# Score banks in a rotation of three, maxima by half in three single banks, values and side stages at exchanged steps

## Chip, cores and metric

One core of a Trainium2 chip runs the whole kernel. The metric is the device time of one execution in microseconds, over several runs; lower is better.

## What is computed

The input is 16 images of 128 channels by 32 x 32 pixels, fp32. Three blocks follow each other, each added to its input: a frequency-gated channel scaling, an attention over the 1024 pixels of an image (8 heads of 16, every token to every token, plus a fixed decaying mix over positions), and a mixture of 8 experts of which each token takes two. The change lies in the attention, which in the reference is:

```
qkvt = x @ W_qkv
q, k, v, t = map(to_heads, jnp.split(qkvt, 4, axis=-1))
dots = jnp.einsum('bhid,bhjd->bhij', q, k) * scale
attn1 = jax.nn.softmax(dots, axis=-1)
out1 = jnp.einsum('bhij,bhjd->bhid', attn1, v)
...
out2 = jnp.einsum('ij,bhjd->bhid', attn2, t)
return concatenated(out1, out2) @ W_out + b_out
```

The softmax subtracts each row's maximum before the exponential, so each row of 1024 dots is needed twice: once for its maximum, once for its exponentials.

## The kernel before

The program is written out by hand for five engines, each with its own instruction stream and semaphores between them. After a setup it runs one iteration `it` for each image, from -1 to 16, and each iteration has 64 **steps** `s`. The loop over steps stands once for each engine (L956 for TensorE, L1191 for ScalarE, L1552 for VectorE), and constants at L77 to L112 say at which step a stage is done. After that come 71 blocks of the expert stage and a closing sum, which the change leaves alone.

**Scores and exponentials.** Step `s` of image `it` has two score matmuls (`scores`, L867, matmul at L876), each of 128 keys by 512 queries of one head, with the negative maximum of the query as two more rows of the stationary and moving operand. They are written to two PSUM banks, `E_BANK + i` for i = 0, 1. ScalarE takes the exponential of each into `probs` in SBUF (`weights`, L1161, activation at L1167). TensorE issues the scores of step s + 1 within step s, and score i of a step waits until the exponential i of the step before is done (L875).

**Values.** Two steps make a **unit** of four heads. `values` (L880, matmuls at L890) multiplies the unit's four blocks of `probs` by the values of these heads, four matmuls on separate 32-column groups, and accumulates in bank 6 over eight units; ScalarE then copies the bank (`copy_o`, L1170). Values run at odd steps, behind the scores of the next step. At the seven steps of `AT_VALUES` they are split into two halves of 256 columns, one in the odd step and one in the even step after it.

**Maxima.** Forty steps ahead (`LEAD`), the scores are computed a first time with queries and keys exchanged (`full_scores`, L848, matmul at L855), 128 queries by 1024 keys in two halves of one bank each. Four banks hold two such units, `M_BANK + 2 * (n % 2) + c`. VectorE reduces the 1024 columns with one instruction (`maximum`, L1411, at L1417) into a column of `row_max`, and TensorE waits for the maximum two units back before it refills the banks (L854). A score and a half of the full scores lie in different row halves of the array, are issued one behind the other and run side by side; I call the two a **pair**. A step has two pairs.

When 32 units are done, `turn_maxima` (L861) transposes `row_max` on TensorE, VectorE negates and splits it (`shift`, L1420), and SyncE moves it with four DMAs into the row of the stacked queries (`load_shift`, L521). The scores of the group wait for that (L873): steps 0 and 32 of an image. `AT_MAX1` is the step at which the second group is turned, `AT_MAX0` that of the next image's first.

**Side stages.** One PSUM bank (`SIDE_BANK`, 7) serves all the other work of an image one after the other, in the order that `side_order` (L126) makes from the constants: transposes of x, the normalised x back, projections to q, k, v and z for the image after next or the next, transposes of the attention output, its projection, transposes for the second norm, gate logits, dispatch counts. TensorE does a stage at its step; ScalarE copies it out `LAG` = 2 steps later (one stage a step earlier), or VectorE reads it. VectorE also does scans for the position mix (`fade_forward`, `fade_backward`), moments, the choice of experts (`choose`, steps `AT_PICK`) and, on TensorE's logits, `logits_out` at `AT_LOGITS`. GpSimd normalises, splits q and k, and sends the tokens out by indirect DMA.

Each engine works strictly in the order of its stream, so a step's stage stands behind that step's pairs on TensorE, behind its exponentials on ScalarE and behind its maximum on VectorE.

## Time and profile before

| | us |
|---|---|
| median of 3 runs | 2412.41 |
| lowest, highest | 2411.95, 2437.68 |
| span of the profiled execution | 2663.0 |
| TensorE busy in it | 2213.5 |
| VectorE busy | 1836.0 |
| ScalarE busy | 1494.7 |
| GpSimd busy | 1021.2 |

Of the profiled execution no other time than its span is listed. The span goes from the first to the last instruction; what lies around it is not shown. It is 251 us longer than the median of the runs. Busy times are unions of what the profiler recorded; a matmul's end is modelled, and matmuls overlap, so TensorE's work is better read from the distance of successive starts. Images start about 117 us apart in it; the expert stage and the closing sum take the last 620 us.

### The profile page before, as it was taken

The page shows a single profiled execution, that of the slowest core. Times are in us where ns is not written, and L with a number is a line of the kernel's source. Part 1 is how long each engine was busy: PE and PEld are TensorE (multiplying, and loading weights), DVE is VectorE, ACT ScalarE, POOL GpSimd, SP SyncE. Part 2 cuts the span into 40 slices and gives each one's busy share as a digit, 9 for nine tenths or more (in the row PEclk, how much of TensorE's full clock was granted, in tenths as well). Part 3 has the DMA queues.
Part 4 walks back from the last instruction along what each step waited for, and adds up shares of the span by engine and source line. Part 5 has one row for each costly group of instructions (what it writes and reads, how often), then busy time and mean ns, then how long its engine had stood idle before and what let it go on. Part 6 is the DMA issues. An engine that isn't in the chain of part 4 may idle for free.

```text
span 2663.0 us, 35930 instructions
## 1 busy us (share of the span) xinstructions
PE 2213.5 (83%) x12448; PEld 985.6 (37%) x12448; DVE 1836.0 (69%) x2613; ACT 1494.7 (56%) x2897; POOL 1021.2 (38%) x1479
## 2 busy tenths in 40 slices
PE   2789998999989999998989999998897277676744
PEld 1333333333324333333434333333332255555633
DVE  5767887877878787888878778787731455555532
ACT  1147877767667676767767676766653033333320
POOL 2202224434241433424143432431404465655564
PEclk9969999989989898999999888898965588878765
DMA  5311223121222212122221212220102366555549
GB/s 167 55 25 25 36 55 89 34 49 40 45 51 51 58 29 54 36 47 48 56 59 29 53 36 47 43 55 26 49 1 93 121 231 191 168 161 168 167 139 345
DMA packets 100989, 215.11 MB, mean 81 GB/s; under 512 B 30224, under 2 KB 50392, under 8 KB 100376
## 3 DMA queue, kind: packets, MB, share of 16 engines
q1 hardware_dynamic: 78000, 166.96, 25.2%
q0 software_dynamic: 17280, 35.95, 3.9%
q10 hardware_dynamic: 5528, 9.91, 1.1%
q8 instruction: 99, 1.62, 0.3%
q14 instruction: 82, 0.67, 0.1%
HBM read 104.30 MB, written 61.23 MB: 62 GB/s over the span
## 4 chain that ended last, share of the span: by engine, by line
PE 63%; ACT 11%; another core or an unknown queue 7%; issue 7%; DMA 4%; POOL 4%; DVE 2%; SPq 1%; ACTq 1%; POOLq 0%; DVEq 0%
PE ps L876 27%; PE ps L890 19%; ACT region L1167 6%; PE ps L833 3%; DMA region<-y_dram 2%; PE ps L841 1%; PE ps L855 1%; PE ps L845 1%; PE ps L910 1%; PE ps L1019 1%; PE ps L1021 1%; POOL y_dram L763 1%; PE ps L923 1%; PE ps L899 1%
## 5 line engine op out<-in xcount | busy, mean ns | idle before, releaser
L1417 DVE TENSOR_REDUCE row_max<-ps 128x1 f32<-128x1024 f32 x1024 | 1235.4, 1216 | 347.2 <-PE ps L855 224.1
L1167 ACT ACTIVATE region<-ps 128x512 f32<-128x512 f32 x2048 | 1116.8, 596 | 566.1 <-PE ps L876 491.1
L876 PE MATMUL ps<-big 50*128 50x512 f32 x2048 | 889.8, 503 | 105.7 <-ACT region L1167 74.6
L855 PE MATMUL ps<-big 48*128 48x512 f32 x2048 | 887.7, 502 | 20.4 <-DMA big<-k_parts 14.8
L876 PEld LDWEIGHTS ps<-big 50*128 50x128 f32 x2048 | 361.2, 200 | 826.4 <-ACT region L1167 650.2
L890 PE MATMUL ps<-region 128*32 128x512 f32 (+1 forms) x4992 | 637.3, 586 | 0.7 <-ACT region L1167 0.7
L855 PEld LDWEIGHTS ps<-big 48*128 48x128 f32 x2048 | 362.7, 202 | 44.5 <-DVE row_max L1417 25.6
L763 POOL DMA_INDIRECT y_dram<-region x284 | 272.6, 960 | 201.5 <-ACT region L1251 123.0
L708 POOL DMA_INDIRECT xs_dram<-region,slot x256 | 249.7, 975 | 80.8 <-issue 71.7
L1019 PE MATMUL ps<-big 128*128 128x512 f32 x284 | 139.4, 491 | 110.9 <-DMA big<-w_dram 39.4
L693 POOL TENSOR_TENSOR region<-region 128x256 f32<-128x256 f32 x64 | 44.8, 732 | 446.1 <-DVE region L1463 446.1
L890 PEld LDWEIGHTS ps<-region 128*32 128x32 f32 x4992 | 102.4, 113 | 201.8 <-issue 200.4
L1243 ACT ACTIVATE region<-ps,big 128x512 f32<-128x512 f32 x71 | 49.0, 690 | 213.7 <-remote 132.1
L644 POOL TENSOR_TENSOR norm_v<-norm 128x8 f32<-128x8 f32 x32 | 6.8, 212 | 406.1 <-DVE norm L1407 406.1
L658 POOL TENSOR_TENSOR region<-region,norm_v 128x256 f32<-128x256 f32 x256 | 155.3, 638 | 6.6 <-POOL norm_v L652 2.9
L1634 DVE TENSOR_TENSOR big<-ps,big 128x512 fp32r<-128x512 f32 x71 | 48.9, 689 | 146.5 <-ACT big L1237 78.3
L1644 DVE TENSOR_SCALAR big<-ps,big 128x512 fp32r<-128x512 f32 x142 | 105.6, 744 | 62.8 <-remote 28.6
L1021 PE MATMUL ps<-big 128*128 128x512 f32 x284 | 127.9, 450 | 0.0
L1020 PE MATMUL ps<-big 128*128 128x512 f32 x284 | 127.8, 450 | 0.0
L1019 PEld LDWEIGHTS ps<-big 128*128 128x128 f32 x284 | 61.4, 216 | 148.4 <-ACT region L1243 60.5
L1647 DVE SCALAR_TENSOR_TENSOR big<-ps,big 128x512 fp32r<-128x512 f32 x142 | 106.6, 751 | 5.0
L1251 ACT ACTIVATE region<-ps,region 128x128 f32<-128x128 f32 x284 | 81.1, 374 | 27.5 <-remote 22.5
(182 smaller groups left out, 2019.2 us busy)
## 6 DMA issues: line engine op xcount, KB each, us to landing
big<-w_dram SPq DMA_DIRECT2D x71, 514.0 KB
big<-q_parts SPq DMA_DIRECT2D x384, 64.0 KB, 2.4
big<-k_parts SPq DMA_DIRECT2D x372, 64.0 KB, 2.4
region<-xs_dram SPq DMA_DIRECT2D x71, 264.0 KB
region<-y_dram SPq DMA_DIRECT2D x16, 1024.0 KB, 9.9
region<-in_x SPq DMA_DIRECT2D x28, 512.0 KB, 5.3
t_dram<-region SPq DMA_DIRECT2D x16, 512.0 KB, 3.4
out<-region ACTq DMA_DIRECT2D x16, 512.0 KB, 5.9
```

Of the source, the lines that this page charges most:

```text
L658: last = pool.tensor_tensor(some, some, v[:, row, t:t + 2].unsqueeze(2).broadcast_to([P, 2, P]), op)
L708: pool.indirect_dma_start(xs_dram[:, :], bass.IndirectOffsetOnAxis(ap=slot[:, n * TILES + t:n * TILES + t + 1], axis=0), n2_row[:, t, :], ...
L763: pool.indirect_dma_start(y_dram[:, :], bass.IndirectOffsetOnAxis(ap=xs[b % XS_BUFS][:, j, INDEX_COL:INDEX_COL + 1].bitcast(I32), axis=0), ...
L855: mm = pe.matmul(ps[:, M_BANK + 2 * (n % 2) + c, :], lane_rows(q_stack[k % 2], h, SHIFT_ROW)[:, t * P:(t + 1) * P], lane_rows(k_stack[k % ...
L876: pe.matmul(ps[:, E_BANK + i, :], lane_rows(k_stack[k % 2], h, STACK)[:, t * P:(t + 1) * P], lane_rows(q_stack[k % 2], h, STACK)[:, c * BA ...
L890: mm = pe.matmul(ps[32 * r:32 * r + 32, O_BANK, cols], v_aug[k % 2][:, t, g * GROUP + r, :], probs[:, u % 2, r, cols], start=(t == 0), sto ...
L1019: pe.matmul(dst, w[:, high_at:high_at + P], high, start=start, stop=False)
L1020: pe.matmul(dst, w[:, high_at:high_at + P], low, start=False, stop=False)
L1021: return pe.matmul(dst, w[:, low_at:low_at + P], high, start=False, stop=stop)
L1167: act.activation(probs[:, u % 2, step_head(k, s, i), :], ps[:, E_BANK + i, :], ACT.Exp, scale=DH ** -0.5).then_inc(exp_done, 1)
L1417: dve.tensor_reduce(row_max[:, h * TILES + t:h * TILES + t + 1], ps[:, at:at + 2, :], AX.XY, ALU.max).then_inc(max_done, 1)
L1647: dve.scalar_tensor_tensor(h_low[b % 2][f], src, w[:, NEG_B1 + f:NEG_B1 + f + 1], h_high[b % 2][f].bitcast(F32), ALU.max, ALU.subtract).th ...
```

## The change

The scores rotate through three banks (0 to 2), counted over all scores, and a score waits for the exponential three before it. The full scores rotate through three single banks (3 to 5), counted by half, and each half waits for the maximum three halves before it. VectorE reduces each half by itself into one of two columns, and joins the two columns with one `tensor_tensor` for each 32 units; `turn_maxima` waits for the join. Values run at even steps, whole, for the unit that ended with the step before, with a wait for its exponentials; the last unit of an image runs in step 0 of the next. Side stages move to odd steps, mostly one step later, some elsewhere; `LAG` is 1, and VectorE's moments keep their distance of 3 steps. The output copies move to the odd steps 17, 33, 49 and 1.

```diff
-AT_MAX1, AT_MAX1_FIRST = 26, 23
-AT_TURN_O3 = 4
-AT_BACK_O = (6, 8)
-AT_PREP = ((0, 2), (14, 16), (18, 20), (22, 24))
-AT_PREP_LATE = ((24, 26), (36, 38), (40, 42), (44, 46))
+AT_MAX1, AT_MAX1_FIRST = 27, 23
+AT_TURN_O3 = 5
+AT_BACK_O = (7, 9)
+AT_PREP = ((1, 3), (15, 17), (19, 21), (23, 25))
+AT_PREP_LATE = ((25, 27), (37, 39), (41, 43), (51, 55))
...
-AT_OUT = (32, 36)
+AT_OUT = (33, 37)
...
-AT_TURN_T2 = (42, 44)
-AT_LOGITS = 53
-AT_TURN_O = (48, 50, 52)
-AT_VZ = (54, 56, 58, 60)
-AT_VZ_FIRST = (24, 26, 28, 30)
-AT_DISPATCH = 62
-AT_VALUES = (10, 12, 28, 30, 38, 40, 46)
-LAG = 2
+AT_TURN_T2 = (41, 43)
+AT_LOGITS = 51
+AT_TURN_O = (31, 47, 53)
+AT_VZ = (45, 49, 59, 61)
+AT_VZ_FIRST = (27, 28, 29, 30)
+AT_DISPATCH = 63
+AT_COPY_O = (17, 33, 49)
+AT_COPY_O3 = 1
+LAG, MOMENT_LAG = 1, 3
...
-AT_GAP = 62
-AT_PICK = (54, 55, 56, 57, 58, 59, 60)
-AT_GATES = 63
-AT_AFFINE = 49
+AT_GAP = 60
+AT_PICK = (52, 53, 54, 55, 56, 57, 58)
+AT_GATES = 62
+AT_AFFINE = 48
...
-        row_max = sb("row_max", [P, STEPS])
+        row_max = sb("row_max", [P, HALVES, STEPS])
...
-        E_BANK, M_BANK, O_BANK, SIDE_BANK = 0, 2, 6, 7
+        E_BANK, M_BANK, O_BANK, SIDE_BANK = 0, 3, 6, 7
+        E_BANKS, M_BANKS = 3, 3
...
-                if unit >= 2:
-                    pe.wait_ge(max_done, unit - 1)
-                mm = pe.matmul(ps[:, M_BANK + 2 * (n % 2) + c, :],
+                half = HALVES * unit + c
+                if half >= M_BANKS:
+                    pe.wait_ge(max_done, half - M_BANKS + 1)
+                pe.matmul(ps[:, M_BANK + half % M_BANKS, :],
...
-                if c == HALVES - 1:
-                    mm.then_inc(full_ready, 1)
...
-                pe.wait_ge(max_done, k * STEPS + (g + 1) * GROUP_ROWS)
+                pe.wait_ge(max_joined, GROUPS * k + g + 1)
...
-                if k * STEPS + s:
-                    pe.wait_ge(exp_done, 2 * (k * STEPS + s) - 1 + i)
-                pe.matmul(ps[:, E_BANK + i, :], lane_rows(k_stack[k % 2], h, STACK)[:, t * P:(t + 1) * P],
+                score = 2 * (k * STEPS + s) + i
+                if score >= E_BANKS:
+                    pe.wait_ge(exp_done, score - E_BANKS + 1)
+                pe.matmul(ps[:, E_BANK + score % E_BANKS, :], lane_rows(k_stack[k % 2], h, STACK)[:, t * P:(t + 1) * P],
...
+                pe.wait_ge(exp_done, 2 * (k * STEPS + 2 * (u + 1)))
...
-                    if here and s % 2:
-                        values(it, s // 2, 0 if s + 1 in AT_VALUES else None)
-                    if here and s in AT_VALUES:
-                        values(it, s // 2 - 1, 1)
+                    if here and s and s % 2 == 0:
+                        values(it, s // 2 - 1)
+                    if post and s == 0:
+                        values(it - 1, UNITS - 1)
...
-                    act.activation(probs[:, u % 2, step_head(k, s, i), :], ps[:, E_BANK + i, :], ACT.Exp,
+                    score = 2 * (k * STEPS + s) + i
+                    act.activation(probs[:, u % 2, step_head(k, s, i), :], ps[:, E_BANK + score % E_BANKS, :], ACT.Exp,
...
-                    if s == 0 and post:
+                    if s == AT_COPY_O3 and post:
                         copy_o(it - 1, 3)
-                    if here and s in (16, 32, 48):
-                        copy_o(it, s // 16 - 1)
+                    if here and s in AT_COPY_O:
+                        copy_o(it, AT_COPY_O.index(s))
...
-                    for c, late in enumerate((LAG, LAG - 1)):
-                        if prep and s == at_k[c] + late:
-                            projected("k", it + 2, c, k_f, k_parts)
+                    if prep and s - LAG in at_k:
+                        projected("k", it + 2, at_k.index(s - LAG), k_f, k_parts)
...
-                dve.wait_ge(full_ready, k * STEPS + n + 1)
-                at = M_BANK + 2 * (n % 2)
                 h, t = max_unit(n)
-                dve.tensor_reduce(row_max[:, h * TILES + t:h * TILES + t + 1], ps[:, at:at + 2, :], AX.XY,
-                                  ALU.max).then_inc(max_done, 1)
+                for c in range(HALVES):
+                    half = HALVES * (k * STEPS + n) + c
+                    dve.wait_ge(full_ready, half + 1)
+                    dve.tensor_reduce(row_max[:, c, h * TILES + t:h * TILES + t + 1], ps[:, M_BANK + half % M_BANKS, :],
+                                      AX.X, ALU.max).then_inc(max_done, 1)
+                if (n + 1) % GROUP_ROWS == 0:
+                    rows = slice(n + 1 - GROUP_ROWS, n + 1)
+                    dve.wait_ge(max_done, HALVES * (k * STEPS + n + 1))
+                    dve.tensor_tensor(row_max[:, 0, rows], row_max[:, 0, rows], row_max[:, 1, rows],
+                                      ALU.max).then_inc(max_joined, 1)
```

## Rows read from the trace of the kernel before

**Rows 1.** Page, part 1: busy time, share of the span, instructions.
```profile
PE 2213.5 (83%) x12448; PEld 985.6 (37%) x12448; DVE 1836.0 (69%) x2613; ACT 1494.7 (56%) x2897; POOL 1021.2 (38%) x1479
```

**Rows 2.** Page, part 4: the chain that ended last, by engine and by line.
```profile
PE 63%; ACT 11%; another core or an unknown queue 7%; issue 7%; DMA 4%; POOL 4%; DVE 2%; SPq 1%; ACTq 1%; POOLq 0%; DVEq 0%
PE ps L876 27%; PE ps L890 19%; ACT region L1167 6%; PE ps L833 3%; DMA region<-y_dram 2%; PE ps L841 1%; PE ps L855 1%; PE ps L845 1%; PE ps L910 1%; PE ps L1019 1%; PE ps L1021 1%; POOL y_dram L763 1%; PE ps L923 1%; PE ps L899 1%
```

**Rows 3.** Busy time by window: images 1 and 7, and a late stretch of image 15.
```profile
core 0: us, PE busy (x) PEld busy (x) DVE busy (x) ACT busy (x) POOL busy (x), PEclk, DMA share, GB/s
274.00:382.00 108.00, 104.35 (x685) 40.28 (x689) 94.13 (x128) 82.89 (x156) 25.57 (x48) 0.98 0.22 41
...
969.00:1086.00 117.00, 109.62 (x683) 41.36 (x685) 93.85 (x131) 83.01 (x156) 43.51 (x73) 0.93 0.23 47
...
1960.00:2010.00 50.00, 49.31 (x198) 19.98 (x198) 5.65 (x16) 23.21 (x44) 15.38 (x16) 0.50 0.11 43
```

**Rows 4.** Timeline, TensorE, image 1: start, length, what (times in us).
```profile
273.97 0.47 PE L876 MATMUL ps<-big 50*128 50x512 f32 x1 [0.54 <-ACT region L1167]
...
274.80 1.06 PE L890 MATMUL ps<-region 128*32 128x512 f32 x8
275.79 0.50 PE L876 MATMUL ps<-big 50*128 50x512 f32 x1
...
276.13 0.39 PE L876 MATMUL ps<-big 50*128 50x512 f32 x1
...
276.46 0.66 PE L821 MATMUL ps<-ident,region 128*128 128x128 f32 x4
277.07 0.49 PE L876 MATMUL ps<-big 50*128 50x512 f32 x1
...
277.99 1.06 PE L890 MATMUL ps<-region 128*32 128x512 f32 x8
...
290.37 0.64 PE L890 MATMUL ps<-region 128*32 128x256 f32 x8
...
381.02 0.47 PE L876 MATMUL ps<-big 50*128 50x512 f32 x1
```

**Rows 5.** Timeline, ScalarE, image 1, steps 8 to 10 (idle before in brackets).
```profile
287.00 1.09 ACT L1167 ACTIVATE region<-ps 128x512 f32<-128x512 f32 x2 [0.22 <-PE ps L876]
...
288.80 1.08 ACT L1167 ACTIVATE region<-ps 128x512 f32<-128x512 f32 x2 [0.22 <-PE ps L876]
290.11 1.09 ACT L1167 ACTIVATE region<-ps 128x512 f32<-128x512 f32 x2 [0.22 <-PE ps L876]
```

**Rows 6.** Timeline, VectorE, image 1, maxima (the second row holds two).
```profile
286.56 1.21 DVE L1417 TENSOR_REDUCE row_max<-ps 128x1 f32<-128x1024 f32 x1
...
288.07 2.33 DVE L1417 TENSOR_REDUCE row_max<-ps 128x1 f32<-128x1024 f32 x2
```

**Rows 7.** Page and groups by line: busy, mean ns, idle before.
```profile
L1174 ACT ACTIVATE region<-ps 128x512 f32<-128x512 f32 x64 | 38.3, 598 | 32.7 <-PE ps L890 32.4
...
L1475 DVE SCALAR_TENSOR_TENSOR region<-ps,b_out,region 128x512 f32<-128x512 f32 x32 | 23.3, 729 | 29.0 <-PE ps L910 29.0
...
L1407 DVE BATCH_NORM_STATS2 norm<-region 128x6 f32<-128x128 f32 x256 | 60.3, 279 | 27.9 <-ACT region L1155 27.9
```

**Rows 8.** Timeline, TensorE and VectorE, image 8, around the logits.
```profile
1183.04 1.95 PE L923 MATMUL ps<-gate_c,region 128*128 128x8 f32 x16
...
1185.03 0.22 DVE L1490 TENSOR_TENSOR gate<-ps,norm_v 128x64 f32<-128x64 f32 x1 [1.31 <-PE ps L923]
```

**Rows 9.** Timeline, image 1: turn of maxima, shift DMAs, score of step 32.
```profile
319.82 0.41 PE L864 MATMUL ps<-ident,row_max 128*32 128x128 f32 x2
...
321.77 2.67 SPq L526 DMA_DIRECT2D big<-max_parts  x4
...
325.75 0.18 PEld L876 LDWEIGHTS ps<-big 50*128 50x128 f32 x1 [0.49 <-DMA big<-max_parts]
```

**Rows 10.** Timeline, TensorE, image 1: second back-transposition.
```profile
301.28 0.63 PE L828 MATMUL ps<-ident,region 128*128 128x128 f32 x4 [0.63 <-ACT region L1121]
```

More of the change, by code:

```diff
@@ L404, in build @@
         max_done = sem("max_done")
-        max_step = sem("max_step")
+        max_joined = sem("max_joined")
         max_split = sem("max_split")
@@ L852, in full_scores @@
                     pe.wait_ge(stack_in[k % 2][h // GROUP], (k // 2 + 1) * STACK_INC)
-                if unit >= 2:
-                    pe.wait_ge(max_done, unit - 1)
-                mm = pe.matmul(ps[:, M_BANK + 2 * (n % 2) + c, :],
-                               lane_rows(q_stack[k % 2], h, SHIFT_ROW)[:, t * P:(t + 1) * P],
-                               lane_rows(k_stack[k % 2], h, SHIFT_ROW)[:, c * BANK:(c + 1) * BANK], start=True, stop=True)
-                if c == HALVES - 1:
-                    mm.then_inc(full_ready, 1)
+                half = HALVES * unit + c
+                if half >= M_BANKS:
+                    pe.wait_ge(max_done, half - M_BANKS + 1)
+                pe.matmul(ps[:, M_BANK + half % M_BANKS, :],
+                          lane_rows(q_stack[k % 2], h, SHIFT_ROW)[:, t * P:(t + 1) * P],
+                          lane_rows(k_stack[k % 2], h, SHIFT_ROW)[:, c * BANK:(c + 1) * BANK], start=True,
+                          stop=True).then_inc(full_ready, 1)
             def turn_maxima(k, g):
-                pe.wait_ge(max_done, k * STEPS + (g + 1) * GROUP_ROWS)
+                pe.wait_ge(max_joined, GROUPS * k + g + 1)
                 pe.wait_ge(side_free, side_at["max", k, g])
-                pe.matmul(ps[0:GROUP_ROWS, SIDE_BANK, 0:P], row_max[:, g * GROUP_ROWS:(g + 1) * GROUP_ROWS], ident[:, :],
+                pe.matmul(ps[0:GROUP_ROWS, SIDE_BANK, 0:P], row_max[:, 0, g * GROUP_ROWS:(g + 1) * GROUP_ROWS], ident[:, :],
                           start=True, stop=True).then_inc(side_ready, 1)
@@ L873, in scores, with values @@
                     pe.wait_ge(shift_in, (2 * k + g + 1) * SHIFT_INC)
-                if k * STEPS + s:
-                    pe.wait_ge(exp_done, 2 * (k * STEPS + s) - 1 + i)
-                pe.matmul(ps[:, E_BANK + i, :], lane_rows(k_stack[k % 2], h, STACK)[:, t * P:(t + 1) * P],
+                score = 2 * (k * STEPS + s) + i
+                if score >= E_BANKS:
+                    pe.wait_ge(exp_done, score - E_BANKS + 1)
+                pe.matmul(ps[:, E_BANK + score % E_BANKS, :], lane_rows(k_stack[k % 2], h, STACK)[:, t * P:(t + 1) * P],
                           lane_rows(q_stack[k % 2], h, STACK)[:, c * BANK:(c + 1) * BANK], start=True,
                           stop=True).then_inc(score_ready, 1)
-            def values(k, u, part=None):
-                g, c, t = u // 16, u // 8 % 2, u % TILES
-                cols = slice(0, BANK) if part is None else slice(part * BANK // 2, (part + 1) * BANK // 2)
+            def values(k, u):
+                g, t = u // 16, u % TILES
                 if u == 0:
                     pe.wait_ge(side_free, side_at["vz", k, 3] + 1)
-                if u == UNITS - 1 and k == IMAGES - 1:
-                    pe.wait_ge(exp_done, 2 * IMAGES * STEPS)
+                pe.wait_ge(exp_done, 2 * (k * STEPS + 2 * (u + 1)))
                 if t == 0 and 4 * k + u // TILES:
@@ L889, in values @@
                 for r in range(GROUP):
-                    mm = pe.matmul(ps[32 * r:32 * r + 32, O_BANK, cols], v_aug[k % 2][:, t, g * GROUP + r, :],
-                                   probs[:, u % 2, r, cols], start=(t == 0), stop=(t == TILES - 1))
-                if part != 0:
-                    mm.then_inc(value_done, 1)
+                    mm = pe.matmul(ps[32 * r:32 * r + 32, O_BANK, :], v_aug[k % 2][:, t, g * GROUP + r, :],
+                                   probs[:, u % 2, r, :], start=(t == 0), stop=(t == TILES - 1))
+                mm.then_inc(value_done, 1)
             def turn_o(k, n):
@@ L1572, in _ @@
                     for quarter in range(4):
-                        if prep and s == at_turn[quarter // 2] + LAG + 1 + quarter % 2:
+                        if prep and s == at_turn[quarter // 2] + MOMENT_LAG + quarter % 2:
                             if quarter == 0:
@@ L1590, in _ @@
                     for quarter in range(4):
-                        if post and s == AT_TURN_T2[quarter // 2] + LAG + 1 + quarter % 2:
+                        if post and s == AT_TURN_T2[quarter // 2] + MOMENT_LAG + quarter % 2:
                             if quarter == 0 and it >= 2:
```

## The prediction, made before the change was run

> **What bounds the kernel now.** I read the busy shares, then the chain of waits, then windows by image, then the timelines of TensorE, ScalarE and VectorE in a quiet stretch. Busy shares put TensorE first [rows 1], and the chain runs 63% through it and 11% through ScalarE, with the score matmuls (L876, 27%) and the values (L890, 19%) ahead [rows 2]. The windows show that the share is not one engine's own work. Image 1 (274 to 382 us) has VectorE busy 94 of 108 us, ScalarE 83, the clock at 0.98 of full; image 7 has the same 94 and 83 busy but takes 117 us at 0.93 [rows 3]. So the instructions are the same and the waits are not. Image 1, from its first score at 273.97 to the next image's at 381.02, takes 107.05 us [rows 4]; I use it as the image with the fewest irregular waits. From 1960 on (image 15, no maxima left) the clock stands at half, 1.2 GHz [rows 3]; I forecast nothing there or in image 0.
>
> TensorE's own need is read from start to start [rows 4]. A pair (score and maximum side by side) starts 0.33 after the one before it (275.79, 276.13, 276.46). A whole unit of values takes 0.99 (274.80 to 275.79), a side stage of four transposes 0.61 (276.46 to 277.07). After that stage the next two pairs run from 277.07 to the values at 277.99: 0.92 where two pairs need 0.67. That is the loop of the two score banks: an exponential must end before its bank's next score can start, and ScalarE stands idle 0.22 before each pair of exponentials, with pairs 1.31 and 1.80 apart where two exponentials need 1.0 [rows 5].
>
> Over an image: 64 steps of two pairs, 128 x 0.333 = 42.6; 32 units of values at 1.0, 32.0; stages 20.9 (12 of transposes at 0.59, ten projections at about 1.07, logits 1.88 [rows 8], two turns of maxima at 0.3, dispatch 0.7; the last figures are from start-to-start in the same timelines). Sum 95.5; the seven values that are split today cost 0.57 a half (0.64 long, and the whole takes 0.07 less than its length [rows 4]) instead of 0.5, 1.0 in all, so 96.5 before. Of image 1's 107.05, TensorE thus waits some 10.5.
>
> VectorE: maxima that follow each other start 1.12 apart (the two at 288.07 take 2.33 together, one takes 1.21) [rows 6], say 1.13: 64 x 1.13 = 72.3. With 94 busy, the rest is about 20.5.
>
> **The change part by part.**
> *Score banks, two to three.* A score now waits for the exponential three before it. Today's loop (exponential 0.6, 0.1 to the score, 0.58 to its result) carries two exponentials, 1.3; with three banks it carries three, 0.43 each, under ScalarE's own 0.49. In a unit with a transposing stage the lost 0.25 [rows 4] goes; about 12 such units: -3.0. The projections of q and k wait 0.46 for ScalarE's copies, three times in image 1, and an output copy (L1174) holds ScalarE 0.5 for the values, four times an image (32.7 us in 64 [rows 7]); with a third bank ahead most of both goes: -2.3. In units without a stage the next limit is late: a maximum or exponential of an even step (0.68), 0.1, a pair 0.33, the values 1.0, result 0.58, together 2.68; the split values hold these at about 2.73 today, so nothing is gained there.
>
> *Values at even steps, whole.* The explicit wait for the unit's exponentials is met, since they were of the step before: 0. Behind the values on TensorE's queue stand the next scores; they have 0.49 more slack than today. Seven splits go: -1.0.
>
> *Maxima in halves, three single banks.* The trace has no 512-wide reduce. An operation that reads every column once lasts 0.279 at 128 columns [rows 7] and 1.21 at 1024 [rows 6], 1.04 ns a column, so a half lasts 1.21 - 0.53 = 0.68; with the same overlap as whole ones (0.08) halves start 0.60 apart. Bounds: half of 1.12, 0.56, with no fixed cost (nothing excludes it by the trace); and 0.73, the other 512-wide operation from PSUM [rows 7]. I take 0.60, by the rows of the reduce itself. Two halves cost 1.20 against 1.13: 64 x 0.07 = +4.5; two joins, each a wait for the last half (0.1) and an operation of 0.2: +0.6. VectorE then needs 92.8 + 5.1 = 97.9 an image, more than TensorE's 95.5. Bounds of VectorE's sum: 128 x 0.56 + 21.1 = 92.8 and 128 x 0.73 + 21.1 = 114.5. For it, VectorE starts after the first half rather than after both, and may lag TensorE by about 1.0 us (two halves, less the round trip) before a full matmul waits; today 0.2.
> The reader sees in rows 6 that a reduce starts before its predecessor has ended. The Trainium skill (VectorE: DVE Perf Modes, "The DRAIN you can't avoid") says that the next operation does not start until the pipe is empty; by that rule the halves would stand 0.68 apart and the third rival below would hold. It adds that operations which are not held start earlier, which is what these rows show.
>
> *Where VectorE's lag is not absorbed.* Around the logits TensorE is taken for 1.88 and VectorE idles 1.31 before L1490 [rows 8]; then the choosing steps add 0.5 each to two halves (each two operations of about 0.25), and the shift 0.65. From step 52 to 57 VectorE needs 6 x 1.20 + 6 x 0.5 + 0.6 (scaling) + 0.65 = 11.4, TensorE 12 pairs, three values and two short stages, with the loop 8.2, and VectorE catches up only from 59: the difference of 3.2 less the 1.0 of slack is +2.2. Two bursts of moments and scaling: +0.3. Scans and copies leave VectorE just below TensorE elsewhere; +0.6 for what the sums don't see.
>
> *Side stages to odd steps, LAG 1.* TensorE's sum is the same; a copy now comes one step after its stage, which ScalarE has room for (83 of 107 busy [rows 3]). The move of the first maxima turn from step 26 to 27 is a loss: in image 1 the turn starts at 319.82, the four DMAs leave from 321.77 to 324.44 and the score of step 32 starts at 325.75, 5.9 later, after 0.49 of waiting for the DMA [rows 9]. Half reduces bring the shift about 0.3 earlier, 5.6; TensorE's work in between is now 4.3 to 4.6 (two values and three steps of pairs, and the loop): it waits 1.0 to 1.3, +0.7. GpSimd's first normalisation starts one step later and is asked for one step later: 0. SyncE's queue keeps its order; its shift DMAs leave a step later, and nothing behind them is near its due time: 0. The exponential of the gap on ScalarE keeps its two steps behind VectorE; if VectorE lags, up to 0.3.
>
> *Sum.* Gains: -3.0 - 2.3 - 1.0, and -0.6 for the second back-transposition, which in image 1 waits 0.63 for the copy of the first because that stands behind an output copy [rows 10]; the two copies now lie in different steps. Losses: 2.2 + 0.3 + 0.6 + 0.7 + 0.3 = 4.1. Together -2.8, say -3.0 an image, and image 1 would take 104 where it takes 107; over images 1 to 14 that is -42 us. Of the profiled execution the page lists no time but the span, 2663.0: the change would make it 2621. The median of the runs is 2412.41, 251 less. Image 7 against image 1 shows that ten us an image are irregular waits, and I take these to be mostly absent from the timed runs, so the 42 come off the median whole: 2412 - 42 = **2370**.
>
> **Rivals.**
> 1. VectorE's lag never binds, TensorE's work and the 2.68 units alone count: 98.5 an image against image 1's 105.5 (its 107.05 less about 1.5 for the clock, 0.98 of full in that window [rows 3]): -7 x 14 = -98, 2314. For it: buffers of halves. Against: VectorE's 97.9 is within 1% of this. Chance 0.12.
> 2. No smoothing between units: in each pair of steps the slower of VectorE and TensorE counts. Summed over the 32 units that is 105 against 105.5: 2405, between 2395 and 2430 as the loops are rounded. For it: only three halves of slack. Chance 0.20.
> 3. The change does what it says for the scores, but VectorE becomes the bound: a half that must wait for its own signal does not start before its predecessor's end. 128 x 0.68 + 21.1 = 108, plus 4 of waits that VectorE cannot fill (logits, shift), 112 against 107: +5 x 14 = +70, 2482. It decides from halves 0.64 apart on, where VectorE's sum with these 4 reaches 107. Place: L1417's successor after. Against: successors with a met wait start early today [rows 6]. Chance 0.18.
> The forecast has 0.50, with 2340 to 2400 as its own range.
>
> **How the numbers follow.** One per cent, 24 us, is about what a measurement of this kernel can tell from no change. Faster than 2388: most of the forecast (0.43) and the first rival, 0.55. Slower than 2436: the third rival and a little of the second, reduced by its own near end, 0.18. The rest 0.27. The range leaves out the far half of the third rival and little of the first: 2305 to 2445.
>
> **What would show it.** Right: scores' pairs 0.33 apart after a stage; ScalarE's 0.22 before exponentials gone in units with a stage; L1417 at 0.68 mean, 0.60 from start to start, VectorE over 0.93 busy in an image; about 1 us of waiting for max_parts before step 32's score; TensorE waiting for row_max near the choosing steps. Wrong: halves 0.68 apart, or TensorE's waits for row_max over 4 us an image (then rival 2 or 3), or none (rival 1). A clock that stays at 2.4 GHz in images 0 or 15, where before it is at 1.2, would add a gain that I have not counted.

## The result, and the profile after

The change made the kernel 0.6% faster where 1.7% was forecast: 2408.4 us (median of 20 runs) against 2422.4 us of the kernel before in the same rounds (20 runs), ratio 0.9938, interval 0.9919 to 0.9958. That is inside the one per cent that the prediction called "the same"; the forecast of 2370 us failed, and the second rival's 2405 us came out.

The profiled execution of the kernel before (span 2663.0 us) is a poor partner for a comparison, so that kernel was profiled again (run before_again below, span 2425.6); the changed kernel's span is 2408.8. The busy shares and the chain of the changed kernel, to be read beside [rows 1, 2], and below them the chain of before_again:

```profile
PE 2077.7 (86%) x11552; PEld 959.4 (40%) x11552; DVE 1906.1 (79%) x3669; ACT 1458.6 (61%) x2897; POOL 1019.7 (42%) x1479
...
PE 58%; DVE 15%; POOL 9%; DMA 7%; issue 6%; ACT 3%; ACTq 1%; SPq 1%; POOLq 0%; DVEq 0%
PE ps L879 21%; PE ps L891 18%; DVE row_max L1418 10%; POOL y_dram L765 6%; PE ps L858 4%; PE ps L835 3%; DMA y_dram<-region 2%; DMA big<-w_dram 2%; ACT region L1168 2%; DMA region<-y_dram 2%; PE ps L843 2%; PE ps L847 1%; PE ps L923 1%; PE ps L899 1%; PE ps L830 1%
```

```profile
PE 60%; ACT 10%; POOL 9%; DMA 7%; issue 7%; DVE 3%; SPq 2%; ACTq 1%; POOLq 0%; DVEq 0%
```

From before_again to the changed kernel ScalarE went from 10% of the chain to 3%, VectorE from 3% to 15%, 10% of it the maxima (L1418): one wait has been exchanged for another. The windows (images 1, 4 and 15), for [rows 3]:

```profile
core 0: us, PE busy (x) PEld busy (x) DVE busy (x) ACT busy (x) POOL busy (x), PEclk, DMA share, GB/s
277.00:383.00 106.00, 103.10 (x614) 40.54 (x612) 97.20 (x192) 80.99 (x154) 25.40 (x48) 0.97 0.21 41
598.00:703.00 105.00, 102.10 (x626) 40.67 (x623) 98.43 (x197) 80.86 (x155) 43.53 (x73) 1.00 0.26 52
...
1759.00:1867.00 108.00, 100.39 (x523) 38.83 (x525) 47.97 (x107) 74.30 (x139) 38.02 (x49) 0.82 0.20 74
```

VectorE is busy 98 of 105 us of an image, as computed. What waits for what in images 4 to 7 (waiting engine and line, releaser, us in total, times, longest):

```profile
PEld ps L879 <- ACT region L1168: 124.1, 194, 1.6
...
PEld ps L858 <- DVE row_max L1418: 22.9, 51, 0.9
...
DVE row_max L1418 <- PE ps L858: 19.9, 48, 1.2
...
PE ps L858 <- DVE row_max L1418: 6.4, 15, 0.6
...
PEld ps L879 <- DMA big<-max_parts: 3.6, 4, 1.1
```

TensorE waits (22.9 + 6.4) / 4 = 7.3 us an image for VectorE to free a bank of maxima; in before_again such waits came to 0.2 us in four images. The prediction had set 4 us as the mark for its being wrong. The waits for max_parts, 0.9 an image, are the "about 1" it gave to the turn at step 27.

The timelines answer to [rows 4 to 6, 9]. First TensorE around two side stages of image 4, and ScalarE beside it:

```profile
601.25 0.66 PE L823 MATMUL ps<-ident,region 128*128 128x128 f32 x4
601.84 0.50 PE L879 MATMUL ps<-big 50*128 50x512 f32 x1
...
602.18 0.39 PE L879 MATMUL ps<-big 50*128 50x512 f32 x1
...
602.50 1.06 PE L891 MATMUL ps<-region 128*32 128x512 f32 x8
```

```profile
602.50 1.08 ACT L1168 ACTIVATE region<-ps 128x512 f32<-128x512 f32 x2
...
605.54 1.11 ACT L1168 ACTIVATE region<-ps 128x512 f32<-128x512 f32 x2
```

Behind a stage the pairs are 0.34 apart and the values follow at 0.66, where they took 0.92 before; ScalarE's 0.22 in front of such exponentials is gone. So the first gain is there. VectorE's halves, and the shift:

```profile
704.74 3.68 DVE L1418 TENSOR_REDUCE row_max<-ps 128x1 f32<-128x512 f32 x6 [0.24 <-DVE base L1542]
...
711.18 0.47 DVE L1407 BATCH_NORM_STATS2 norm<-region 128x6 f32<-128x128 f32 x2
711.63 1.29 DVE L1418 TENSOR_REDUCE row_max<-ps 128x1 f32<-128x512 f32 x2
```

```profile
641.85 0.41 PE L866 MATMUL ps<-ident,row_max 128*32 128x128 f32 x2
...
643.64 2.42 SPq L528 DMA_DIRECT2D big<-max_parts  x4
...
647.72 0.18 PEld L879 LDWEIGHTS ps<-big 50*128 50x128 f32 x1 [0.84 <-DMA big<-max_parts]
```

Six halves take 3.68 and one 0.68, so they start (3.68 - 0.68) / 5 = 0.60 apart. Length and spacing are those of the prediction, and the third rival (0.68 apart) is out. The groups of the costliest lines, for [rows 7]:

```profile
L1418 DVE TENSOR_REDUCE row_max<-ps 128x1 f32<-128x512 f32 x2048 | 1293.6, 682 | 141.2 <-PE ps L858 127.7 <-DVE base L1542 3.8 <-DVE max_parts L1432 3.6
...
L1175 ACT ACTIVATE region<-ps 128x512 f32<-128x512 f32 x64 | 38.5, 601 | 17.2 <-PE ps L891 17.0
```

and the output copies, the second of them, in before_again:

```profile
L1174 ACT ACTIVATE region<-ps 128x512 f32<-128x512 f32 x64 | 38.3, 598 | 21.7 <-PE ps L890 21.3
```

The output copies' waits for values fell from 21.7 us to 17.2; the 32.7 of [rows 7] belong to the execution of 2663 us. Now the place where the loss is seen best, VectorE's steps 57 and 58 of image 4 (timeline, VectorE and TensorE):

```profile
692.39 1.29 DVE L1418 TENSOR_REDUCE row_max<-ps 128x1 f32<-128x512 f32 x2
692.52 0.39 PE L879 MATMUL ps<-big 50*128 50x512 f32 x1
693.14 0.18 PEld L858 LDWEIGHTS ps<-big 48*128 48x128 f32 x1 [0.66 <-DVE row_max L1418]
...
693.60 0.27 DVE L1431 TENSOR_SCALAR max_parts<-ps 32x128 fp32r<-32x128 f32 x1
693.90 0.28 DVE L1432 SCALAR_TENSOR_TENSOR max_parts<-ps,max_parts 32x128 fp32r<-32x128 f32 x1
...
694.42 0.22 DVE L1512 TENSOR_REDUCE gate_v<-gate 128x8 f32<-128x64 f32 x1 [0.24 <-DVE max_parts L1432]
694.67 0.23 DVE L1513 TENSOR_TENSOR pick<-rank,gate_v 128x64 f32<-128x64 f32 x1
694.90 0.39 PE L879 MATMUL ps<-big 50*128 50x512 f32 x1
695.04 1.29 DVE L1418 TENSOR_REDUCE row_max<-ps 128x1 f32<-128x512 f32 x2
...
695.79 0.18 PEld L858 LDWEIGHTS ps<-big 48*128 48x128 f32 x1 [0.94 <-DVE row_max L1418]
```

Shift and choosing keep VectorE from its next half from 693.7 to 695.04. The full-score half that should run beside the score of 694.90 waits for its bank and starts at 695.79, 0.9 us behind it; the projection, scores and values behind it in TensorE's queue wait with it.

### The profile page after: what moved, and what is told of

Its sections match the earlier page's. It is cut to its first block, busy times and chain, and to the rows that moved or that the text cites. A ratio compares the mean times of both kernels' runs of the same rounds, so it can differ in the third digit from the quotient of the medians.

```text
span 2408.8 us, 35243 instructions
## 1 busy us (share of the span) xinstructions
PE 2077.7 (86%) x11552; PEld 959.4 (40%) x11552; DVE 1906.1 (79%) x3669; ACT 1458.6 (61%) x2897; POOL 1019.7 (42%) x1479
## 4 chain that ended last, share of the span: by engine, by line
PE 58%; DVE 15%; POOL 9%; DMA 7%; issue 6%; ACT 3%; ACTq 1%; SPq 1%; POOLq 0%; DVEq 0%
PE ps L879 21%; PE ps L891 18%; DVE row_max L1418 10%; POOL y_dram L765 6%; PE ps L858 4%; PE ps L835 3%; DMA y_dram<-region 2%; DMA big<-w_dram 2%; ACT region L1168 2%; DMA region<-y_dram 2%; PE ps L843 2%; PE ps L847 1%; PE ps L923 1%; PE ps L899 1%; PE ps L830 1%
## 5 line engine op out<-in xcount | busy, mean ns | idle before, releaser
L1418 DVE TENSOR_REDUCE row_max<-ps 128x1 f32<-128x512 f32 x2048 | 1293.6, 682 | 141.2 <-PE ps L858 127.7
L1168 ACT ACTIVATE region<-ps 128x512 f32<-128x512 f32 x2048 | 1095.0, 601 | 409.3 <-PE ps L879 403.1
L858 PE MATMUL ps<-big 48*128 48x512 f32 x2048 | 836.4, 479 | 48.8 <-DVE row_max L1418 31.4
L879 PE MATMUL ps<-big 50*128 50x512 f32 x2048 | 776.2, 463 | 32.8 <-ACT region L1168 22.5
L879 PEld LDWEIGHTS ps<-big 50*128 50x128 f32 x2048 | 327.0, 192 | 663.0 <-ACT region L1168 493.4
L891 PE MATMUL ps<-region 128*32 128x512 f32 x4096 | 574.6, 634 | 0.0
L858 PEld LDWEIGHTS ps<-big 48*128 48x128 f32 x2048 | 347.6, 194 | 151.5 <-DVE row_max L1418 121.6
L1019 PE MATMUL ps<-big 128*128 128x512 f32 x284 | 125.5, 442 | 76.8 <-DMA big<-w_dram 76.2
L891 PEld LDWEIGHTS ps<-region 128*32 128x32 f32 x4096 | 82.1, 110 | 165.6 <-issue 83.1
L1650 DVE TENSOR_SCALAR big<-ps,big 128x512 fp32r<-128x512 f32 x142 | 105.7, 744 | 34.2 <-PE ps L1021 33.7
L1020 PE MATMUL ps<-big 128*128 128x512 f32 x284 | 117.4, 413 | 0.0
L1021 PE MATMUL ps<-big 128*128 128x512 f32 x284 | 116.9, 412 | 0.0
L1069 PE MATMUL ps<-ident,region 128*128 128x128 f32 x128 | 31.5, 428 | 61.3 <-POOL region L772 61.3
```

Source lines behind the costliest of these rows:

```text
L858: pe.matmul(ps[:, M_BANK + half % M_BANKS, :], lane_rows(q_stack[k % 2], h, SHIFT_ROW)[:, t * P:(t + 1) * P], lane_rows(k_stack[k % 2], h, ...
L879: pe.matmul(ps[:, E_BANK + score % E_BANKS, :], lane_rows(k_stack[k % 2], h, STACK)[:, t * P:(t + 1) * P], lane_rows(q_stack[k % 2], h, ST ...
L891: mm = pe.matmul(ps[32 * r:32 * r + 32, O_BANK, :], v_aug[k % 2][:, t, g * GROUP + r, :], probs[:, u % 2, r, :], start=(t == 0), stop=(t = ...
L1019: pe.matmul(dst, w[:, high_at:high_at + P], high, start=start, stop=False)
L1020: pe.matmul(dst, w[:, high_at:high_at + P], low, start=False, stop=False)
L1021: return pe.matmul(dst, w[:, low_at:low_at + P], high, start=False, stop=stop)
```

## Experiments

"An image" below is the time from the first exponential of image 1 to that of image 15, by 14; in the two kernels that matter most these are

```profile
277.25 0.60 ACT L1168 ACTIVATE region<-ps 128x512 f32<-128x512 f32 x1 [5.00 <-PE ps L879]
...
1759.26 0.60 ACT L1168 ACTIVATE region<-ps 128x512 f32<-128x512 f32 x1 [0.84 <-PE ps L879]
```

in the changed kernel, and in before_again

```profile
269.61 0.60 ACT L1167 ACTIVATE region<-ps 128x512 f32<-128x512 f32 x1 [0.22 <-PE ps L876]
...
1763.77 0.60 ACT L1167 ACTIVATE region<-ps 128x512 f32<-128x512 f32 x1 [0.50 <-PE ps L876]
```

so 1482.0 / 14 = 105.9 us and 1494.2 / 14 = 106.7 us. The same lines of the two kernels with light maxima below, the changed one and the one before, give 99.2 and 105.8:

```profile
261.98 0.60 ACT L1168 ACTIVATE region<-ps 128x512 f32<-128x512 f32 x1 [5.37 <-PE ps L879]
...
1650.23 0.60 ACT L1168 ACTIVATE region<-ps 128x512 f32<-128x512 f32 x1 [0.84 <-PE ps L879]
```

```profile
256.96 0.60 ACT L1167 ACTIVATE region<-ps 128x512 f32<-128x512 f32 x1 [0.22 <-PE ps L876]
...
1737.56 0.60 ACT L1167 ACTIVATE region<-ps 128x512 f32<-128x512 f32 x1 [0.50 <-PE ps L876]
```

Each of these is one execution, and the clock that TensorE was granted differs from image to image: 1.00 (2.4 GHz) in some, 0.95 to 0.98 on average in others, most of which last 1 to 4 us longer. Of images 2 to 13 those with 1.00 alone have medians of 105.7 in before_again, 104.6 in the changed kernel (two images), 98.1 in its light form and 105.5 in that of the kernel before, so the clock is not what sets these four apart.

All runs (ratio to the kernel before, timed beside each):

| kernel | median us | ratio (95%) | an image, us |
|---|---|---|---|
| before_again | 2427.4 (one run) | | 106.7 |
| changed kernel | 2408.4 | 0.9938 (0.9919-0.9958) | 105.9 |
| after_half_columns | 2300.4 | 0.9509 (0.9479-0.9538) | 99.2 |
| before_half_columns | 2402.3 | 0.9926 (0.9899-0.9953) | 105.8 |
| two_score_banks_four_maxima_banks | 2463.8 | 1.0179 (1.0153-1.0205) | 109.3 |
| schedule_alone | 2472.6 | 1.0215 (1.0191-1.0238) | 109.2 |
| halves_alone | 2417.2 | 0.9993 (0.9967-1.0020) | 106.7 |
| third_bank_old_order | 2402.6 | 0.9916 (0.9885-0.9946) | 105.3 |
| third_bank_old_order_half_columns | 2323.1 | 0.9583 (0.9543-0.9622) | 101.2 |
| scans_spread | 2389.7 | 0.9895 (0.9852-0.9938) | 105.3 |
| scans_left_out | 2373.9 | 0.9805 (0.9754-0.9857) | 104.3 |
| turn_at_26 | 2401.3 | 0.9919 (0.9888-0.9951) | 105.4 |
| addition_moved | 2402.9 | 0.9922 (0.9892-0.9952) | 105.0 |
| addition_moved_scans_spread | 2385.7 | 0.9833 (0.9792-0.9874) | 104.3 |
| four_pieces | 2422.3 | 0.9999 (0.9969-1.0029) | 107.1 |
| all_reliefs | 2395.3 | 0.9906 (0.9875-0.9937) | 104.8 |
| choosing_earlier | 2392.2 | 0.9866 (0.9824-0.9908) | 104.7 |

### Light maxima, in both kernels

```diff
-  ps[:, M_BANK + half % M_BANKS, :],           AX.X    # changed kernel
+  ps[:, M_BANK + half % M_BANKS, 0:BANK // 2], AX.X
-  ps[:, at:at + 2, :],           AX.XY                 # kernel before
+  ps[:, at:at + 2, 0:BANK // 2], AX.XY
```

> The changed kernel, with each maximum taken over 256 of the 512 columns of its bank; the maxima of the other half of the columns are left out, every matmul and every exponential stays. A reduce is then about 0.41 us long instead of 0.68, and VectorE has some 34 us less an image (128 x 0.27). Theory V (VectorE became the bound: it has 98 of the 105 to 106 us of an image, and TensorE waits 7 us for its banks): the waits of TensorE for row_max go and the image falls to TensorE's own 95.5 and 2 to 4 of waits for exponentials, so 97.5 to 99.5 us, and the time to some 2409 - 14 x 7 = 2310 us (2285 to 2335). Rival S (the score loop, the side stages and the wait for the shifts hold the image; the waits for row_max only stand where TensorE would wait anyway): the image stays at 104 or above, 2385 us or more.

> The kernel before, with each maximum taken over 2 x 256 of its 2 x 512 columns; the maxima of the other columns are left out. The reduce falls from 1.13 us to some 0.6. Theory V says that VectorE was not the bound here (no waits for row_max to speak of in image 1): 2385 to 2415 us, at most 2 us an image less. Rival W (VectorE bound the kernel before as well, and what the change gained is something else): it falls as much as the changed kernel does with the same relief, by 80 us or more, to 2335 us or less.

The changed kernel fell by 4.3 points of its ratio, the kernel before by 0.7. Waits over four images, changed kernel with light maxima:

```profile
DVE row_max L1418 <- PE ps L858: 112.1, 191, 1.9
...
PEld ps L858 <- DVE row_max L1418: 1.1, 4, 0.3
```

and the kernel before with them, below it before_again:

```profile
PEld ps L876 <- ACT region L1167: 158.5, 316, 1.1
```

```profile
PEld ps L876 <- ACT region L1167: 156.6, 306, 1.2
```

In the first it is VectorE that waits now, and TensorE's waits for it went from 29.3 to 1.1 us. In the second the wait for exponentials is what it was in before_again (156.6 us). So the part of VectorE's work that was left out costs the changed kernel 105.9 - 99.2 = 6.7 us an image, and the kernel before 106.7 - 105.8 = 0.9. Theory V holds, rival S and rival W are out; and since the kernel before reads half the columns too and gains little, shorter reads of PSUM as such are not what the changed kernel gained. Between the two light kernels lies what banks and order give TensorE: 6.6 us an image.

### Where the 6.7 us lie

Both kernels share one order of steps, so their steps can be set side by side (time from the first exponential of a pair of steps to that of the next pair, median of images 2 to 13, us):

```
steps        light maxima   changed
8, 9             2.91         3.61
30, 31           3.06         3.79
36, 37           2.66         3.27
56, 57           2.66         3.65
58, 59           2.66         3.65
60, 61           3.71         4.37
all 64          99.1        105.7
```

By stretches the difference is 1.7 in steps 0 to 15 (behind the moments, the scaling and the first scans), 0 in 16 to 27, 2.0 in 28 to 41 (scans, shift, scaling, additions), 0 in 42 to 49 and 2.9 in 50 to 61 (choosing and shift).

### The parts alone

Two score banks and four banks of halves in the new order; the new order with the old banks and whole reduces; the halves with the old order and banks; halves and three score banks with the old order.

```diff
-  E_BANK, M_BANK, ... = 0, 3, 6, 7;  E_BANKS, M_BANKS = 3, 3
+  E_BANK, M_BANK, ... = 0, 2, 6, 7;  E_BANKS, M_BANKS = 2, 4
```

> The changed kernel with two score banks and four banks for the halves of the maxima, everything else as changed. VectorE may then be four halves behind (1.6 us) instead of three (1.0), and the score loop loses its third bank. If the third bank is worth the 3.0 us an image of the prediction and the deeper lag nothing: 2409 + 42 = 2450 us (2435 to 2465). If VectorE is the bound by its mean load alone, neither matters: 2400 to 2420 us. If the lag is what decides, the waits for row_max fall from 7.3 to under 4 us an image and it is faster: 2360 to 2395 us.

> The kernel before with the new order of the steps alone: values whole at even steps, side stages at odd steps, but two score banks, pairs of banks for the maxima and one reduce of 1024 columns a unit. VectorE has 4.5 us an image less than in the changed kernel (64 x 1.13 against 128 x 0.60 and a join). Theory V: the schedule's own gain (seven split values 1.0 us, one of the waits of the copies) comes without VectorE's cost: 14 x 2 to 3 us below the kernel before, 2375 to 2390 us. Rival E (the third score bank is what makes the new order possible, ScalarE's copies would otherwise hold both banks): not faster than before, 2415 us or more.

> The kernel before with its old order of steps and its two score banks, its four banks of maxima used as single banks of 512 columns with one reduce each and a join at the end of a group. VectorE goes from 94 to 98.6 us an image. The images of the kernel before with light maxima took 105.3 us, so VectorE's cost is hidden up to some 6.5 us: if halves only add load, 2418 + 14 x 0 to 2, 2410 to 2450 us. If a first half that is reduced half a unit earlier gives back more than the load costs: under 2410 us.

> The kernel before with halves, three score banks and three banks for the maxima as in the change, but its old order of steps: values at odd steps, right behind the scores of the next step, seven of them split, side stages at even steps. The values now state the wait for their own exponentials that the two-bank scores implied. If the third bank pays only when TensorE does not meet the values of a step before its exponentials are done (theory O: bank and order are worth something together only, since the order alone cost 2% and the halves alone nothing), the loop is as long as before and VectorE's three halves of cover bind at the choosing: 2405 to 2440 us. If the bank itself is the gain: 2390 us or less.

The new order without the third bank loses 2%, with halves (1.0179, near the 2450 us that the third bank's price gave) or without (1.0215): the waits of the former, four images,

```profile
PEld ps L879 <- ACT region L1168: 195.4, 337, 1.7
...
PEld ps L858 <- DVE row_max L1418: 1.1, 4, 0.4
```

show TensorE's waits for exponentials up from 124.1 to 195.4, and none to speak of for VectorE, which with four halves of cover and 109 us an image keeps up. The order alone was expected to gain; it does the reverse, and TensorE's waits for exponentials there are 186.9 us in four images against 156.6 in before_again, so the loop of two banks is held up more than in the old order. That it is ScalarE's copies that hold it is rival E's reading, not shown by itself. Halves alone change nothing. The third bank in the old order is as fast as the whole change (0.9916 against 0.9938, the intervals overlap). Its 2402.6 us lies outside both answers, but nearer theory O's, and O's reason fell: the bank pays without the new order. Both may be held by VectorE, so one more run asked what the order is worth without that.

> Halves and three score banks in the old order (the run third_bank_old_order), with each maximum over 256 of the 512 columns; the maxima of the other columns are left out. With VectorE out of the way the order shows what it is worth. If the new order gives TensorE something that VectorE's load hides in the changed kernel, this one is well above the 2300 us of the changed kernel with the same relief: 2340 us or more. If order and bank are the same gain, and the bank alone is enough: 2295 to 2315 us.

It came between the two answers: 101.2 us an image against 105.8 (two banks) and 99.2 (bank and order). The third bank with the halves is worth 4.6 us an image of TensorE's time, the new order another 2.0. VectorE hides the second entirely: with full maxima the old order takes 105.3, the new one 105.9.

### Taking work off VectorE, or moving it

```diff
-AT_FORWARD, AT_BACKWARD = tuple(range(8, 24, 2)), tuple(range(28, 44, 2))
+AT_FORWARD, AT_BACKWARD = (1, 3, 9, 12, 15, 18, 21, 24), (26, 29, 32, 35, 39, 42, 49, 60)   # scans_spread
-  forward[:, at:at + PIECE], ...
+  forward[:, at:at + 2], ...                                                                # scans_left_out
-PIECES = 8
+PIECES = 4                                                                                  # four_pieces
```

> The changed kernel with the same 16 scans an image (532 ns each), no longer at every second step of 8 to 22 and 28 to 42 but three to four steps apart over steps 1 to 60, and GpSimd's addition of their result moved behind its second normalising. Nothing is left out; VectorE's load of an image stays 98 us. If VectorE's lag is a matter of the place (two steps with a scan want 2 x 1.26 + 0.53 = 3.05 us against TensorE's 2.98, and three halves ahead are 1.0 us of cover), the waits for row_max fall from 7.3 to 4 to 5 us an image and the time to 2409 - 14 x 2.5 = 2374 us (2350 to 2392). If VectorE's sum of an image alone decides (98 busy and the turns that nothing hides), the place does not matter: 2400 to 2420 us.

> The changed kernel with each scan over 2 columns instead of 128; the recurrence over the other columns is left out, all instructions and waits stay. VectorE has about 16 x 0.43 = 7 us an image less, at steps 8 to 42 only. If VectorE bounds the image by its sum, or by its lag in these steps, they now run at TensorE's pace and the steps from 44 to 63 stay as they are: 3 to 5 us an image less, 2340 to 2370 us. If the loss lies at the moments and the choosing (steps 44 to 58) alone, as the prediction had it for 2.2 of its us: at most 1 us an image, 2395 us or more.

> The changed kernel with each recurrence in four pieces of 256 columns, one at every fourth step, instead of eight of 128 at every second. Nothing is left out. A scan of 128 columns took 532 ns and one of 2 columns 280, so some 0.28 us stand in every piece and one of 256 columns should take 0.79: VectorE has 8 x (2 x 0.53 - 0.79) = 2.2 us an image less. In the run with the scans left out 3.1 us less of VectorE gave 1.6 us an image, so by the same share 1.1 us: 2408 - 15 = 2393 us (2385 to 2400). If a burst of 0.79 us costs more at its place than the sum gives back: 2405 us or more.

The same scans spread out gave 0.4 points, some 10 us of the 35 expected if place alone decided, and its interval overlaps that of the changed kernel; TensorE's waits for maxima fell from 7.3 to 6.2 us an image, not to 4 to 5. Without the scans the image lost 1.6 us of the 3 to 5 expected, and the time, 2373.9, missed both answers, nearer the first; but the relief was smaller than reckoned, as the group of the 2-column scans shows:

```profile
L1457 DVE TENSOR_TENSOR_SCAN region<-fade,region 128x2 f32<-128x2 f32 x32 | 8.8, 275 | 0.0
```

VectorE's busy time fell by 3.1 us an image, so about half of each us came back. Yet four_pieces, with a scan of 256 columns at every fourth step that takes

```profile
L1456 DVE TENSOR_TENSOR_SCAN region<-fade,region 128x256 f32<-128x256 f32 x16 | 12.6, 785 | 0.0
```

785 ns as expected, was no faster than the kernel before, and its interval lies clear of the changed kernel's. VectorE is busy 1.3 us an image less there (the scans alone are 2.3 shorter), so the sum of VectorE's work does not set the time. The burst, 0.79 us at one step for 0.53, makes steps 10 and 11 and steps 30 and 31 0.26 longer each, but other steps get shorter, and the medians of the 32 pairs of steps add up to 105.9 against 105.7. What makes the profiled execution longer is images with a lower granted clock, such as the second of these two, image 5 behind image 4:

```profile
601.40:707.69 106.29, 103.34 (x623) 41.16 (x621) 96.66 (x188) 80.74 (x154) 43.87 (x73) 0.98 0.25 51
707.69:816.34 108.65, 105.60 (x623) 41.53 (x621) 97.15 (x188) 80.85 (x154) 43.87 (x73) 0.95 0.25 50
```

Images at 0.98 take 105.6 to 106.7 us there and 105.5 to 106.3 in the changed kernel. But six of the images 1 to 14 stand at 0.94 or 0.95, with 108.2 to 110.1 us, and one in the changed kernel. Over its 12 runs the mean granted clock is 0.929, over the changed kernel's 20 it is 0.935. So less work on VectorE brought nothing, and why the clock was lower is open.

> The changed kernel with the second turn of the maxima back at step 26. The wait for the shifts before the score of step 32 (0.9 us an image in the profile of the changed kernel) goes, and the turn's 0.2 us stands behind values: 0.5 to 0.9 us an image less, 2395 to 2402 us. If VectorE's lag catches TensorE there instead, no change: 2404 to 2412 us.

turn_at_26 (`AT_MAX1` = 26) halved the wait for max_parts, from 3.6 to 1.7 us in four images; its 0.2 points are inside the intervals.

```diff
-AT_OUT = (33, 37)
+AT_OUT = (11, 13)
...
+  act.activation(t2[:, ...], side, ACT.Identity, bias=b_out[:, 0:1])        # ScalarE
+  pool.tensor_tensor(t2[:, ...], t2[:, ...], x_buf[...][:, ...], ALU.add)   # GpSimd
```

> The changed kernel with the addition of bias and image to the projected attention (two operations of 746 ns an image on VectorE) given to ScalarE (two copies with bias of 0.6 us) and GpSimd (four additions of 0.73 us), and the two projections moved from steps 33 and 37 to the free steps 11 and 13. Nothing is left out. VectorE has 1.5 us less, at steps where it costs the changed kernel some 1.5 us an image against the run with light maxima: 0.5 to 1.2 us an image less, 2388 to 2402 us. If two more copies between exponentials cost as much, or the steps 10 to 13 pay what 33 to 38 save: 2405 us or more.

> The kernel of the run above with the scans at steps 10, 12, 14, 16, 18, 20, 22, 24 and 29, 33, 35, 37, 39, 41, 50, 60, and GpSimd's addition of their result behind its second normalising. Both reliefs together: some 2 to 2.5 us an image below the changed kernel, 2370 to 2382 us, if what is lost is lost at the places where VectorE has extra work. If the sum of VectorE's work alone counts, only the 1.5 us that left it: 2385 to 2395 us.

> The changed kernel with the addition moved off VectorE, four pieces of 256 columns at steps 12, 14, 20, 22 and 24, 35, 39, 52 (where TensorE has a side stage of its own), and the second turn of the maxima at step 26. Nothing is left out. Against the run addition_moved_scans_spread (2386 us) VectorE has 2.2 us an image less: by half of that, with 0.3 us for the turn, 1.4 us an image, 2366 us (2355 to 2378). If the load no longer counts because TensorE's own stages now bound the image (101.2 and 99.2 us with light maxima): no lower than 2380 us.

> The kernel of the run addition_moved_scans_spread with the seven parts of the choosing at steps 52, 52, 53, 53, 54, 55, 56 instead of 52 to 58, one each. Nothing is left out and VectorE's work is the same. In steps 52 and 53 TensorE needs 5.5 us with light maxima (the logits lie there) and VectorE with its maxima, the logits and the scaling 3.4, so 2 us are free; in steps 56 to 61, where the image loses 2.6 us against light maxima, VectorE has some 1.0 us less. If the place decides: 0.7 to 1.5 us an image less, 2365 to 2376 us. If not: 2380 to 2390 us, as before this edit.

The addition moved alone is within the intervals of the changed kernel: it saves 0.5 at steps 36 and 37 and 0.6 at 38 and 39, but the projections make steps 12 to 15 longer (3.37 and 3.37 where 2.77 and 3.09 stood). With the scans spread as well it is the best complete kernel of the study, 0.9833 (0.9792 to 0.9874), clear of the changed kernel. TensorE's waits for maxima are 7.2 us an image even there, so the sum of these waits is not the price. Four pieces at other steps and the turn at 26 lost that again (0.9906), and the choosing at earlier steps gained nothing: steps 60 and 61 fell from 4.37 to 3.75, steps 56 and 57 rose from 3.89 to 4.76. Work moved out of one pair of steps came back in another.

## Why the prediction was wrong, and where it was right

*TensorE's side: right in its sum.* The gains (3.0 + 2.3 + 1.0 + 0.6) less the shift's 0.7 and the gap's 0.3 made 5.9 us an image; the two kernels with light maxima are 6.6 apart. Between bank and order it was less exact: the bank gave 4.6 where 5.3 stood, the order 2.0 where 0.6 was left. The single terms were not measured apart. With the lag out of the way the kernel does what the first rival said: 98.5 and 2314 us there, 99.2 and 2300 here. The turn at step 27 made TensorE wait 0.9 us, near the 1.0 to 1.3 forecast; its price of 0.7 is not shown, since taking the turn back changed the time by less than the intervals.

*The reduce: right.* 0.68 long, 0.60 apart, VectorE 98 us an image. (The 97.9 of the prediction has a small slip: 94 less 72.3 is 21.7, not 20.5.) The rule of the Trainium skill that the prediction set beside it (VectorE: DVE Perf Modes, "The DRAIN you can't avoid") would have had the halves 0.68 apart; these rows differ from it, and 0.60 stands, in line with the page's remark there that an operation that is not held starts earlier.

*The step that failed* is "Where VectorE's lag is not absorbed": 2.2 + 0.3 + 0.6 = 3.1 us was put there, and VectorE's price rose by 6.7 - 0.9 = 5.8. Its largest term was near (2.2 for the choosing; 2.9 in steps 50 to 61). The two small ones, 0.9 for the bursts and for "what the sums don't see", stood for 1.7 + 2.0 = 3.7. The reasoning behind them was that scans and copies leave VectorE just below TensorE and a cover of 1.0 us takes the rest. But TensorE's mean of 95.5 / 32 = 2.98 a pair of steps is not its pace everywhere: in steps 36 and 37 or 56 to 59 it is 2.66 (the table; the prediction itself had 2.68), while a pair with a scan costs VectorE 2 x 1.20 + 0.53 = 2.93. The likely reading is that the cover is used up once, and that behind it such pairs run at VectorE's pace; the slack that TensorE's stages give in steps 16 to 27 comes too late to be spent.

That is close to the second rival's picture, the slower engine counting in each pair of steps, and its 105 an image and 2405 us are what came out (105.9 and 2408). But the picture itself is not shown, and its number is in part luck. If VectorE's busy time in the changed kernel is cut into pairs of steps at the starts of its maxima, and the larger of it and the light kernel's pair is taken each time, the pairs add up to 106.2 or 107.1 us (as the steps of the two engines are set against each other), where 105.7 was measured. The same sum for the kernel before gives 108.6 or 109.1, where 106.3 was measured. By the rule alone the change would thus have gained more than it did. And steps 8 and 9 take 3.61 us, though by this count neither engine needs more than 3.2 there: what is lost shows in other steps than those with the work.

So, per image: -6.6 + 5.8 = -0.8 where the prediction had -2.8, and -12.2 us over images 1 to 14 where it had -42.

*What was not counted.* Image 15, where no maxima are left, took 107.7 us against 116.7 in before_again, at the same granted clock of 0.82: 9 us that the forecast set at nothing. The clock itself gave nothing there. In image 0 it was 1.00 against 0.79, the case that the prediction had named as a gain left out, but both executions took 134.3 us there. 7.7 us more before image 0 and 3.2 less after image 15 make up the difference of the spans, 16.8. The 7.7 come with the banks, three for scores and three for maxima: with full maxima image 0 starts at 142.6 to 144.5 us in every kernel that has them, and at 133.3 to 137.9 in those with two and four.

*What stays open* is a rule for how much of VectorE's work comes back. The sum failed for four_pieces, the place as I reckoned it for choosing_earlier; which steps absorb a burst was only seen, not derived.

## What to carry to other kernels

When two engines share a loop and their sums are within a few per cent, the difference of the sums over a whole stage says little: 95.5 and 97.9 us became 105.9. Adding up the larger of the two for each short stretch came nearer here, but too high for the kernel with the deeper buffer, so it is a first estimate and no more. To price an engine that is about to become the bound, run both kernels with its work made light: the two gaps are its price before and after, and what is left between the light kernels is what the change gives. A buffer in one place can make an accompanying reordering unnecessary, so try it alone.

## What the runs showed of the hardware that I had not expected

A forward scan took 275 ns over 2 columns, 532 over 128 and 785 over 256: 2.0 ns a column and about 0.27 us for each instruction. The half reduces took 682 ns over 512 columns and 418 over 256, so 1.03 ns a column and 0.15 fixed. The Trainium skill (DVE: opcode table, instruction layouts, handler registers and perf-mode slots, "6. Datapath and trigger behaviour") says that the scan runs at half throughput; these rows, 2.0 ns a column against the reduce's 1.03, agree. The fixed part of the scan made "leave it out" a relief of 4.0 us an image by the scans' lengths, 3.1 of VectorE's busy time, where I had reckoned 7.
